# Expert matrices kept interleaved in SBUF, and read by the products with a step of eight values

## The chip, the core and the metric

One core of a Trainium2 chip runs the whole program. The metric is device time in microseconds (us) of one execution, given as the median of several runs. Five engines work beside each other and are tied by semaphores alone: TensorE (PE, with its weight loads listed as PEld), VectorE (DVE), ScalarE (ACT), GpSimd (POOL) and SyncE (SP), which here issues most of the DMAs.

## What is computed

An attention block and a feed-forward block with eight experts, each followed by a layer norm. Only the second half of the program is touched by the change:

```python
x = layernorm(x + attention(x))                  # x: 8 x 512 tokens of 512 values
logits = clip(xt @ gate_w.T)                     # 8 experts
top_w, top_idx = top_k(logits, 2)
rw = softmax(top_w)
deltas = softmax(expert_atom_weights) @ atoms    # 8 x 4096
weighted = deltas * sigmoid(importance)
vals = einsum('tk,tks->ts', rw, weighted[top_idx])
contrib = segment_sum((xt[:, cols] * vals).T, rows)   # rows, cols: from mask_idx
x = layernorm(x + xt @ W.T + contrib.T)
```

The kernel writes the sparse part of each expert into a dense 512 x 512 matrix, together with `W` and the identity, so that a token's result is the sum of two products, one with each chosen expert's matrix, weighted by `rw`.

## The kernel before

The stages run one after the other: `expert_entries` (the sparse entries), `attention` (most of the time; it also routes the tokens of all batches but the last), `experts` and `combine`. The eight experts' matrices lie in DRAM as `expert_weights`, with the expert as the innermost index: for each row and column the values of the eight experts lie side by side.

`experts` has two halves. In the first, the preparation, SyncE loads the matrices into SBUF in eight parts of 128 partitions x 2048 values (256 columns times 8 experts), into a ring of three slots called `stage`. Products are made in float32r, and each factor is split in a high part (the value rounded to float32r) and a low part (the rest), so that three products of parts stand for one. For each part and each expert ScalarE casts 256 values, read from `stage` with a step of eight, into `d_hi` (line 1558), where the experts lie apart; then VectorE (line 1621, function `lows`) or GpSimd (line 1433) subtracts `d_hi` from the same values in `stage` and writes `d_lo`. `DVE_E` (line 1396) shares this: VectorE has four of eight experts in parts 0 to 3 and all of them in parts 4 to 7. A slot of the ring is loaded again when both have finished with it (lines 1412 and 1413).

Between these, VectorE finishes the last 512 tokens: their layer norm, their logits (by TensorE from `x1T`, which ScalarE copies behind part 0), their two best experts, and their places in the table `expert_slots`, which GpSimd scatters in eight small DMAs behind part 3. In the program of VectorE the order is `lows(0)`, logits, `lows(1)`, choice of experts, `lows(2)`, places, `lows(3)`, `lows(4)`, counts of tiles, `lows(5)`, the tiles' experts, `lows(6)`, tile numbers, `lows(7)`, token numbers (line 1707). SyncE loads the table (`slots`, line 1420) when the scatter has landed; the token numbers need it.

The second half is a loop over 72 tiles of 128 tokens of one expert, in turns of four. GpSimd fetches the 128 rows of a tile with an indirect DMA (line 1458) and, for an earlier tile, sends the result's rows with another (line 1464). TensorE turns the fetched rows (four transposes, line 1523); ScalarE and VectorE split them into `xT_hi` and `xT_lo`; TensorE then makes twelve products of 128 x 128 by 128 x 512 (lines 1534 to 1536), whose moving operand is the tile's expert in `d_hi` or `d_lo`, picked by a register; ScalarE scales the result. TensorE turns the next tile's rows ahead of the products of this one. TensorE and GpSimd both enter the loop only when all of `d_lo` is there.

Of the kernel before, what the change touches and what calls it, by code (L numbers as in the profile page):

```python
# [27 lines left out]
P = 128  # L28
# [1310 lines left out]
def experts(nc, sem, s_passed, psum, ident, upper, ones, R, rows, gate_w, d_dram, y_dram):  # L1339

    LAST = NT - TT
    with ExitStack() as ctx:
        def sb(name, shape, dt=F32):
            return ctx.enter_context(nc.sbuf_tensor(name, shape, dt))

        d_hi, d_lo = sb("d_hi", [P, C, NE, DM], F32R), sb("d_lo", [P, C, NE, DM], F32R)

        STAGES = 3
        stage = sb("stage", [P, STAGES, DM * NE // 2])
# [43 lines left out]
        block = ctx.enter_context(nc.Block())  # L1393
        PARTS = 2 * C

        DVE_E = [NE // 2] * (PARTS // 2) + [NE] * (PARTS - PARTS // 2)

        def part(q, e):

            return stage[:, q % STAGES].rearrange("p (r e) -> p e r", e=NE)[:, e]  # L1400

        def place(w, q, e):
            return w[:, q // 2, e, (q % 2) * (DM // 2):(q % 2 + 1) * (DM // 2)]

        @block.sync
        def _(sp):
            sp.dma_start(gate_rows[:], gate_w).then_inc(s_gate_in, 16)
            weights = d_dram[0:DM * DM, :].rearrange("(c p h r) e -> c h p (r e)", c=C, p=P, h=2)
            for q in range(PARTS):
                if q >= STAGES:  # L1410

                    sp.wait_ge(s_d_lo, sum(DVE_E[:q - STAGES + 1]))
                    sp.wait_ge(s_d_lo_pool, NE * (q - STAGES + 1) - sum(DVE_E[:q - STAGES + 1]))
                sp.dma_start(stage[:, q % STAGES], weights[q // 2, q % 2]).then_inc(s_d_in[q % STAGES], 16)
                if q == 3:
                    sp.wait_ge(s_x1, TT)
                    sp.dma_start(R.x1_dram[LAST * P:, :].rearrange("(t p) d -> p t d", p=P), rows[:]).then_inc(s_x1_out, 16)

            sp.wait_ge(R.s_placed, 32 * (NT + 1))
            sp.dma_start(slots[:].rearrange("p n a -> p (n a)"), R.table.rearrange("(p n) a -> p (n a)", p=P)).then_inc(s_ids_in, 16)  # L1420
            for k in range(GROUP):

                sp.wait_ge(s_y_out[k], 16 * TURNS)

        @block.gpsimd
        def _(pool):
# [1 line left out]
            pool.wait_ge(s_var, 1)  # L1428
            pool.tensor_tensor(rstd[:], var_eps[:], R.minus_half[:], ALU.pow).then_inc(s_rstd, 1)
            for q in range(PARTS):  # L1430
                for e in range(DVE_E[q], NE):
                    pool.wait_ge(s_d_hi, q * NE + e + 1)
                    pool.tensor_tensor(place(d_lo, q, e), part(q, e), place(d_hi, q, e).bitcast(F32),
                                       ALU.subtract).then_inc(s_d_lo_pool, 1)
                if q == PARTS // 2 - 1:

                    pool.wait_ge(s_place, 1)
                    for t in range(TT):
                        for k in range(2):
                            pool.indirect_dma_start(  # L1440
                                out=R.table, out_offset=bass.IndirectOffsetOnAxis(ap=place_tile[:, t, k:k + 1], axis=0),
                                in_=last_slot[:, t, k], in_offset=None).then_inc(R.s_placed, 16)

            pool.wait_ge(s_ids, 1)
            pool.wait_ge(s_x1_out, 16)
            pool.wait_ge(s_d_lo, sum(DVE_E))
            pool.wait_ge(s_tiles, 1)

            def fetch(j, k, buf, sent):
# [36 lines left out]
        def _(pe):  # L1486
# [27 lines left out]
            pe.matmul(psum[:, 1, 0:NE], ones[:], before[:, TT], start=True, stop=True).then_inc(s_counts, 1)  # L1514

            pe.wait_ge(s_tiles, 1)
            pe.wait_ge(s_d_lo, sum(DVE_E))
            pe.wait_ge(s_d_lo_pool, NE * PARTS - sum(DVE_E))

            def turn(j, k, loaded):  # L1520
                pe.wait_ge(s_tok_in[k], loaded)
# [4 lines left out]
            def multiply(j, k):  # L1526
                e = pe.value_load(tile_expert_i[0:1, bass.ds(j, 1)], min_val=0, max_val=NE - 1)
                pe.wait_ge(s_lo, j + 1)

                dst = psum[:, 4 + k, :]  # L1530
                for c in range(C):
                    hi = d_hi[:, c, bass.ds(e, 1), :].rearrange("p a n -> p (a n)")
                    lo = d_lo[:, c, bass.ds(e, 1), :].rearrange("p a n -> p (a n)")
                    pe.matmul(dst, xT_hi[:, k % 2, c], hi, start=c == 0, stop=False)
                    pe.matmul(dst, xT_hi[:, k % 2, c], lo, start=False, stop=False)
                    last = pe.matmul(dst, xT_lo[:, k % 2, c], hi, start=False, stop=c == C - 1)
                last.then_inc(s_y, 1)
# [16 lines left out]
        def _(act):  # L1554
            for q in range(PARTS):
                act.wait_ge(s_d_in[q % STAGES], 16 * (q // STAGES + 1))
                for e in range(NE):
                    act.copy(place(d_hi, q, e), part(q, e)).then_inc(s_d_hi, 1)
                if q == 0:
                    for c in range(C):  # L1560
                        act.wait_ge(s_x1T_pe, c + 1)
                        act.copy(x1T[:, c], psum[:, 4 + c, :]).then_inc(s_x1T, 1)
                if q == 2:
                    act.wait_ge(s_gap, 1)
                    act.activation(gap[:, 1], gap[:, 0], ACT.Exp).then_inc(s_gap_exp, 1)
# [25 lines left out]
        def _(dve):  # L1591
# [24 lines left out]

            def lows(q):

                for e in range(DVE_E[q]):
                    dve.wait_ge(s_d_hi, q * NE + e + 1)  # L1620
                    dve.tensor_tensor(place(d_lo, q, e), part(q, e), place(d_hi, q, e).bitcast(F32),
                                      ALU.subtract).then_inc(s_d_lo, 1)

            lows(0)
# [242 lines left out]
```

## Time and profile before

| | us |
|---|---|
| median of three runs | 2079.24 (2078.22 to 2080.32) |
| the profiled execution, its own time | 2079.65 |
| its span in the trace | 2078.1 |
| TensorE busy | 1845.8 (89%) |
| VectorE busy | 1188.1 (57%) |
| ScalarE busy | 816.1 (39%) |
| GpSimd busy | 793.4 (38%) |

The span is what the trace covers, from the first to the last recorded work; the execution's own time is a little longer. Busy times are sums over the whole span, in which the attention takes the greater part; for a change in one stage the stretch of that stage has to be read by itself. The experts' preparation runs from about 1688 to 1755 us, the loop over the tiles from there to 2002, and the combining stage to the end. In the rows, a start is given in us from the span's start; products show some 0.39 us each although they start more closely, since they overlap, so their pace is the distance of starts.

### The profile page before, as it was taken

Reading aid. Unit: us, or ns where it says so; the run is one execution under the profiler, and the core shown is the slowest. Engines: PE = TensorE matmul, PEld = TensorE weight load, DVE = VectorE, ACT = ScalarE, POOL = GpSimd, SP = SyncE. Lnnn points to the kernel's source line nnn. Section 1 sums busy time; section 2 is a strip of 40 time slices with the busy share of each in tenths; the row PEclk is TensorE's granted clock in tenths of the full one; section 3 lists DMA queues with packets and bytes.
Section 4 is the critical chain, followed back from the end, with each engine's and each line's share of the span. In section 5 each row is a group of like instructions: output and inputs, shape, how many; then the busy total and the mean of one; then the engine's idle time right before and its main releaser. Section 6 shows DMA issues by size and latency. Waiting matters only on the chain. (4 is left out here: it accounts for less than half of the span.)

```text
span 2078.1 us, 35224 instructions
## 1 busy us (share of the span) xinstructions
PE 1845.8 (89%) x9447; PEld 1549.2 (75%) x9448; DVE 1188.1 (57%) x3710; ACT 816.1 (39%) x2038; POOL 793.4 (38%) x1242
## 2 busy tenths in 40 slices
PE   6899999999999999999999999999999842999950
PEld 6788788878887888788878887888788732877740
DVE  4445446665666566656656665676567756222237
ACT  1244434434443343444434443444344443333324
POOL 5366423223232333233323332333233333666643
PEclk6899999999999999999999999999999975999975
DMA  9453353323333433243324333333324133444458
GB/s 316 158 167 117 112 190 106 116 98 132 116 106 101 142 101 106 96 142 106 111 94 139 111 104 119 121 107 138 124 74 141 52 122 104 149 156 148 146 210 364
DMA packets 113037, 278.74 MB, mean 134 GB/s; under 512 B 17808, under 2 KB 28064, under 8 KB 103016
## 3 DMA queue, kind: packets, MB, share of 16 engines
q1 hardware_dynamic: 92128, 229.03, 31.7%
q0 software_dynamic: 20816, 48.73, 7.4%
q8 instruction: 26, 0.43, 0.1%
q14 instruction: 67, 0.55, 0.1%
HBM read 207.00 MB, written 70.72 MB: 134 GB/s over the span
## 5 line engine op out<-in xcount | busy, mean ns | idle before, releaser
L847 POOL TENSOR_SCALAR probs<-probs,row_inv 128x128 f32<-128x128 f32 (+3 forms) x512 | 275.7, 584 | 471.3 <-DVE row_inv L1220 466.8
L1127 ACT ACTIVATE probs<-probs,neg_max 128x512 f32<-128x512 f32 (+3 forms) x512 | 283.2, 556 | 410.2 <-DVE neg_max L1212 397.4
L924 PE MATMUL psum<-xT_hi,w_hi 128*128 128x512 f32 x640 | 257.4, 402 | 23.4 <-DVE qT_lo L1233 10.6
L926 PE MATMUL psum<-xT_hi,w_lo 128*128 128x512 f32 x640 | 251.5, 393 | 0.0
L925 PE MATMUL psum<-xT_lo,w_hi 128*128 128x512 f32 x640 | 250.9, 392 | 0.0
L1212 DVE CUSTOM_DVE_ANT_0 probs<-psum,causal 128x512 f32<-128x512 f32 (+3 forms) x512 | 222.8, 487 | 46.5 <-PE psum L926 20.3
L1223 DVE TENSOR_TENSOR pT_lo<-psum,pT_hi 128x512 fp32r<-128x512 f32 (+1 forms) x384 | 206.5, 594 | 9.6 <-ACT pT_hi L1137 9.6
L924 PE MATMUL psum<-wo_hi,oT_hi 128*128 128x512 f32 x512 | 202.7, 396 | 1.4 <-DVE oT_lo L1223 1.4
L926 PE MATMUL psum<-wo_hi,oT_lo 128*128 128x512 f32 x512 | 200.3, 391 | 0.0
L925 PE MATMUL psum<-wo_lo,oT_hi 128*128 128x512 f32 x512 | 199.6, 390 | 0.0
L1137 ACT CAST pT_hi<-psum 128x512 fp32r<-128x512 f32 (+1 forms) x384 | 172.9, 529 | 61.5 <-PE psum L951 61.5
L1233 DVE SCALAR_TENSOR_TENSOR qT_lo<-psum,qT_hi 128x512 fp32r<-128x512 f32 x128 | 88.5, 691 | 169.1 <-ACT qT_hi L1141 169.1
L924 PE MATMUL psum<-kT_hi,qT_hi 128*128 128x512 f32 (+3 forms) x512 | 170.1, 332 | 2.9 <-issue 1.5
L924 PE MATMUL psum<-pT_hi,v_hi 128*128 128x512 f32 (+1 forms) x384 | 142.5, 371 | 26.2 <-DVE xT_lo L352 24.5
L925 PE MATMUL psum<-kT_lo,qT_hi 128*128 128x512 f32 (+3 forms) x512 | 164.9, 322 | 0.0
L924 PEld LDWEIGHTS psum<-xT_hi,w_hi 128*128 128x128 f32 x640 | 120.6, 188 | 59.2 <-DVE qT_lo L1233 13.4
L926 PE MATMUL psum<-kT_hi,qT_lo 128*128 128x512 f32 (+3 forms) x512 | 164.5, 321 | 0.0
L951 PE MATMUL psum<-ident,probs 128*128 128x128 f32 x1280 | 160.7, 273 | 2.6 <-DVE pT_lo L1223 2.6
L951 PEld LDWEIGHTS psum<-ident,probs 128*128 128x128 f32 x1280 | 147.4, 141 | 19.9 <-issue 3.2
L1141 ACT ACTIVATE qT_hi<-psum 128x512 fp32r<-128x512 f32 x128 | 76.2, 596 | 207.8 <-PE psum L926 205.6
L267 DVE CUSTOM_DVE_ANT_0 route_product<-route_rows,route_gate 128x512 f32<-128x512 f32 x224 | 151.2, 684 | 0.0
L1223 DVE TENSOR_TENSOR oT_lo<-psum,oT_hi 128x512 fp32r<-128x512 f32 x128 | 88.4, 691 | 102.0 <-ACT oT_hi L1150 102.0
(248 smaller groups left out, 3813.0 us busy)
## 6 DMA issues: line engine op xcount, KB each, us to landing
w_hi<-split_qk_weights SPq DMA_DIRECT2D x140, 256.0 KB, 2.7
w_lo<-split_qk_weights SPq DMA_DIRECT2D x140, 256.0 KB, 2.9
wo_hi<-split_out_weights SPq DMA_DIRECT2D x28, 1024.0 KB, 5.0
wo_lo<-split_out_weights SPq DMA_DIRECT2D x28, 1024.0 KB, 7.1
c_y<-chosen_rows SPq DMA_DIRECT2D x32, 512.0 KB, 9.1
x_in<-in_L_attn_x_dram SPq DMA_DIRECT2D x8, 1024.0 KB, 6.5
expert_weights<-fill_sb SPq DMA_DIRECT2D x4, 2048.0 KB, 9.2
stage<-expert_weights SPq DMA_DIRECT2D x8, 1024.0 KB, 7.0
```

The lines of the kernel that those rows point to most:

```text
L267: dve.tensor_tensor_reduce(R.product[:, e % 2], R.rows[:], R.gate[:, e], 1.0, 0.0, ALU.mult, ALU.add, R.logits[:, e:e + 1]).then_inc(R.s_c ...
L847: last = pool.tensor_scalar(p, p, row_inv[:, buf, i:i + 1], 1.0, ALU.mult, ALU.mult)
L924: pe.matmul(dst, hi_s, hi_m, start=start, stop=False)
L925: pe.matmul(dst, hi_s, lo_m, start=False, stop=False)
L926: return pe.matmul(dst, lo_s, hi_m, start=False, stop=stop)
L951: last = pe.transpose(psum[:, BANKS_PT[unit], at:at + P], probs[:, buf, src:src + P], ident[:])
L1127: last = act.activation(probs[:, buf, a:a + w], probs[:, buf, a:a + w], ACT.Exp, bias=neg_max[:, buf, i:i + 1], scale=-1.0, accum_out=row_ ...
L1137: act.copy(pT_hi[:, buf, a:z], psum[:, BANKS_PT[u], 0:z - a]).then_inc(s_pt_hi, 1)
L1141: act.mul(qT_hi[:, buf], psum[:, BANK_A, :], SCALE).then_inc(s_q_hi, 1)
L1212: last = dve.tensor_tensor_reduce(probs[:, buf, a:a + w], psum[:, BANK_S + bank, col:col + w], causal[:, T - w:T], -1.0, -MASKED, ALU.add, ...
L1223: dve.tensor_tensor(lo, src, hi.bitcast(F32), ALU.subtract).then_inc(done, 1)
L1233: dve.scalar_tensor_tensor(out=qT_lo[:, buf], in0=psum[:, BANK_A, :], scalar=SCALE, in1=qT_hi[:, buf].bitcast(F32), op0=ALU.mult, op1=ALU. ...
```

## The change

`d_hi` and `d_lo` are laid out like the matrices in DRAM, with the expert innermost. The split then works on whole parts: one cast of 2048 adjacent values on ScalarE, and one subtraction of 2048 adjacent values, on VectorE for parts 0, 2, 4, 5, 6 and 7 and on GpSimd for parts 1 and 3. The waits count parts instead of experts. The products take their 512 moving values from `d_hi` and `d_lo` with a step of eight, beginning at the expert's number. Nothing else is different.

```diff
--- before.py
+++ after.py
@@ -1343,7 +1343,7 @@
         def sb(name, shape, dt=F32):
             return ctx.enter_context(nc.sbuf_tensor(name, shape, dt))
 
-        d_hi, d_lo = sb("d_hi", [P, C, NE, DM], F32R), sb("d_lo", [P, C, NE, DM], F32R)
+        d_hi, d_lo = sb("d_hi", [P, C, DM, NE], F32R), sb("d_lo", [P, C, DM, NE], F32R)
 
         STAGES = 3
         stage = sb("stage", [P, STAGES, DM * NE // 2])
@@ -1393,14 +1393,14 @@
         block = ctx.enter_context(nc.Block())
         PARTS = 2 * C
 
-        DVE_E = [NE // 2] * (PARTS // 2) + [NE] * (PARTS - PARTS // 2)
-
-        def part(q, e):
-
-            return stage[:, q % STAGES].rearrange("p (r e) -> p e r", e=NE)[:, e]
-
-        def place(w, q, e):
-            return w[:, q // 2, e, (q % 2) * (DM // 2):(q % 2 + 1) * (DM // 2)]
+        DVE_PARTS = [q for q in range(PARTS) if q not in (1, 3)]
+
+        def part(q):
+
+            return stage[:, q % STAGES]
+
+        def place(w, q):
+            return w[:, q // 2, (q % 2) * (DM // 2):(q % 2 + 1) * (DM // 2)].rearrange("p r e -> p (r e)")
 
         @block.sync
         def _(sp):
@@ -1409,8 +1409,10 @@
             for q in range(PARTS):
                 if q >= STAGES:
 
-                    sp.wait_ge(s_d_lo, sum(DVE_E[:q - STAGES + 1]))
-                    sp.wait_ge(s_d_lo_pool, NE * (q - STAGES + 1) - sum(DVE_E[:q - STAGES + 1]))
+                    if q - STAGES in DVE_PARTS:
+                        sp.wait_ge(s_d_lo, DVE_PARTS.index(q - STAGES) + 1)
+                    else:
+                        sp.wait_ge(s_d_lo_pool, (1, 3).index(q - STAGES) + 1)
                 sp.dma_start(stage[:, q % STAGES], weights[q // 2, q % 2]).then_inc(s_d_in[q % STAGES], 16)
                 if q == 3:
                     sp.wait_ge(s_x1, TT)
@@ -1428,9 +1430,9 @@
             pool.wait_ge(s_var, 1)
             pool.tensor_tensor(rstd[:], var_eps[:], R.minus_half[:], ALU.pow).then_inc(s_rstd, 1)
             for q in range(PARTS):
-                for e in range(DVE_E[q], NE):
-                    pool.wait_ge(s_d_hi, q * NE + e + 1)
-                    pool.tensor_tensor(place(d_lo, q, e), part(q, e), place(d_hi, q, e).bitcast(F32),
+                if q not in DVE_PARTS:
+                    pool.wait_ge(s_d_hi, q + 1)
+                    pool.tensor_tensor(place(d_lo, q), part(q), place(d_hi, q).bitcast(F32),
                                        ALU.subtract).then_inc(s_d_lo_pool, 1)
                 if q == PARTS // 2 - 1:
 
@@ -1443,7 +1445,7 @@
 
             pool.wait_ge(s_ids, 1)
             pool.wait_ge(s_x1_out, 16)
-            pool.wait_ge(s_d_lo, sum(DVE_E))
+            pool.wait_ge(s_d_lo, len(DVE_PARTS))
             pool.wait_ge(s_tiles, 1)
 
             def fetch(j, k, buf, sent):
@@ -1514,8 +1516,8 @@
             pe.matmul(psum[:, 1, 0:NE], ones[:], before[:, TT], start=True, stop=True).then_inc(s_counts, 1)
 
             pe.wait_ge(s_tiles, 1)
-            pe.wait_ge(s_d_lo, sum(DVE_E))
-            pe.wait_ge(s_d_lo_pool, NE * PARTS - sum(DVE_E))
+            pe.wait_ge(s_d_lo, len(DVE_PARTS))
+            pe.wait_ge(s_d_lo_pool, PARTS - len(DVE_PARTS))
 
             def turn(j, k, loaded):
                 pe.wait_ge(s_tok_in[k], loaded)
@@ -1529,8 +1531,8 @@
 
                 dst = psum[:, 4 + k, :]
                 for c in range(C):
-                    hi = d_hi[:, c, bass.ds(e, 1), :].rearrange("p a n -> p (a n)")
-                    lo = d_lo[:, c, bass.ds(e, 1), :].rearrange("p a n -> p (a n)")
+                    hi = d_hi[:, c, :, bass.ds(e, 1)].rearrange("p n a -> p (n a)")
+                    lo = d_lo[:, c, :, bass.ds(e, 1)].rearrange("p n a -> p (n a)")
                     pe.matmul(dst, xT_hi[:, k % 2, c], hi, start=c == 0, stop=False)
                     pe.matmul(dst, xT_hi[:, k % 2, c], lo, start=False, stop=False)
                     last = pe.matmul(dst, xT_lo[:, k % 2, c], hi, start=False, stop=c == C - 1)
@@ -1554,8 +1556,7 @@
         def _(act):
             for q in range(PARTS):
                 act.wait_ge(s_d_in[q % STAGES], 16 * (q // STAGES + 1))
-                for e in range(NE):
-                    act.copy(place(d_hi, q, e), part(q, e)).then_inc(s_d_hi, 1)
+                act.copy(place(d_hi, q), part(q)).then_inc(s_d_hi, 1)
                 if q == 0:
                     for c in range(C):
                         act.wait_ge(s_x1T_pe, c + 1)
@@ -1616,9 +1617,9 @@
 
             def lows(q):
 
-                for e in range(DVE_E[q]):
-                    dve.wait_ge(s_d_hi, q * NE + e + 1)
-                    dve.tensor_tensor(place(d_lo, q, e), part(q, e), place(d_hi, q, e).bitcast(F32),
+                if q in DVE_PARTS:
+                    dve.wait_ge(s_d_hi, q + 1)
+                    dve.tensor_tensor(place(d_lo, q), part(q), place(d_hi, q).bitcast(F32),
                                       ALU.subtract).then_inc(s_d_lo, 1)
 
             lows(0)
```

## Rows read from the trace of the kernel before

**Rows 1.** Stretches: length, busy PE, PEld, DVE, ACT, POOL, granted clock, DMA share, GB/s.

```profile
15.70:20.00 4.30, 3.69 (x32) 3.60 (x32) 1.78 (x5) 0.39 (x1) 4.30 (x2) 0.50 0.97 394
...
26.50:41.00 14.50, 14.03 (x65) 13.94 (x64) 1.68 (x3) 2.49 (x2) 8.27 (x7) 0.50 0.94 391
...
1690.00:1755.00 65.00, 10.45 (x40) 6.58 (x40) 48.56 (x143) 38.61 (x70) 29.53 (x36) 0.55 0.46 155
1755.90:1758.60 2.70, 2.69 (x6) 2.15 (x7) 0.75 (x2) 0.57 (x1) 1.86 (x5) 0.50 0.40 124
...
1762.00:2002.30 240.30, 231.60 (x1123) 184.83 (x1121) 52.30 (x139) 82.78 (x139) 155.77 (x269) 1.00 0.45 149
```

**Rows 2.** Timeline of TensorE in the loop: start, length, line, operands.

```profile
1757.35 0.63 PE L1534 MATMUL psum<-d_hi,tokT_hi 128*128 x1
...
1757.78 0.63 PE L1535 MATMUL psum<-d_lo,tokT_hi 128*128 x1
...
1795.32 0.60 PE L1523 MATMUL psum<-ident,stage 128*128 128x128 f32 x4
...
1799.20 0.39 PE L1535 MATMUL psum<-d_lo,tokT_hi 128*128 x1
1799.43 0.39 PE L1536 MATMUL psum<-d_hi,tokT_lo 128*128 x1
...
1801.72 0.60 PE L1523 MATMUL psum<-ident,stage 128*128 128x128 f32 x4
```

**Rows 3.** GpSimd's fetches, line 1458, from 1740 to 2003 us.

```profile
L1458 POOL DMA_INDIRECT stage<-x,ids_now x72: 975/986/1027, 1749.1 to 1991.7; - x72
```

**Rows 4.** Instructions by line, 1690 to 2005 us: count | busy us, mean ns | idle before.

```profile
L1534 PE MATMUL psum<-d_hi,tokT_hi 128*128 x288 | 120.0, 417 | 4.2 <-issue 4.2
...
L1464 POOL DMA_INDIRECT chosen_rows<-stage,dest_now x72 | 71.0, 987 | 28.8 <-issue 21.6 <-ACT stage L1582 7.2
...
L1558 ACT CAST d_hi<-stage 128x256 fp32r<-128x256 f32 x64 | 36.2, 653 | 28.6 <-DMA stage<-expert_weights 28.5
...
L1621 DVE TENSOR_TENSOR d_lo<-stage,d_hi 128x256 fp32r<-128x256 f32 x48 | 25.7, 604 | 0.3 <-ACT d_hi L1558 0.3
L1433 POOL TENSOR_TENSOR d_lo<-stage,d_hi 128x256 fp32r<-128x256 f32 x16 | 15.1, 984 | 7.6 <-ACT d_hi L1558 7.6
```

**Rows 5.** Waits from 1756 to 2003 us: total, times, longest.

```profile
PEld psum L1523 <- DMA stage<-x,ids_now: 10.4, 14, 1.6
```

**Rows 6.** Instructions by line, whole span: the same work on adjacent values.

```profile
L607 DVE TENSOR_TENSOR wv_lo<-wo_raw,wv_hi 128x2048 fp32r<-128x2048 f32 x1 | 2.3, 2293 | 0.1
...
L536 ACT CAST wv_hi<-wo_raw 128x2048 fp32r<-128x2048 f32 x1 | 1.9, 1899 | 1.9 <-DMA wo_raw<-in_L_attn_wv_dram 1.9
...
L830 POOL TENSOR_TENSOR v_lo<-v_raw,v_hi 128x512 fp32r<-128x512 f32 x32 | 41.5, 1296 | 6.0 <-POOL v_hi L825 6.0
```

**Rows 7.** Timeline of the preparation: ScalarE, VectorE and SyncE.

```profile
1697.68 2.02 ACT L1562 COPY x1T<-psum 128x512 f32<-128x512 f32 x4
...
1715.51 2.22 DVE L1621 TENSOR_TENSOR d_lo<-stage,d_hi 128x256 fp32r<-128x256 f32 x4 [0.25 <-ACT d_hi L1558]
...
1720.16 6.33 DVE L1621 TENSOR_TENSOR d_lo<-stage,d_hi 128x256 fp32r<-128x256 f32 x12
...
1728.81 4.26 DVE L1621 TENSOR_TENSOR d_lo<-stage,d_hi 128x256 fp32r<-128x256 f32 x8
...
1732.94 0.32 SPq L1420 DMA_DIRECT2D slots<-expert_slots  x1
...
1746.50 0.29 DVE L1707 TENSOR_SCALAR token_ids<-slots 128x256 int32<-128x256 int32 x1
```

**Rows 8.** DMA issues of the page: KB each, median us to landing.

```profile
stage<-expert_weights SPq DMA_DIRECT2D x8, 1024.0 KB, 7.0
```

**Rows 9.** Timeline of weight loads: importance rows (step 32 values) and gate rows (adjacent).

```profile
15.72 3.60 PEld L490 LDWEIGHTS psum<-ident,imp_sb 8*128 8x128 f32 x32 [2.81 <-DMA imp_sb<-in_L_ffn_importance_dram]
...
1689.43 0.50 PEld L1490 LDWEIGHTS psum<-ident,gate_rows 8*128 8x128 f32 x4 [9.10 <-DMA gate_rows<-in_L_ffn_gate_w_dram]
```

## The prediction

> **What bounds the kernel now.** The edit touches one stage, the experts, so I read the stretches first [rows 1]. From 1690 to 1755 us TensorE is busy 10.45 of 65 us while VectorE is busy 48.56: this is the preparation, in which the experts' matrices are split into a high and a low part. From 1762 to 2002.3 us TensorE is busy 231.6 of 240.3 us at the full clock: this is the loop over 72 token tiles. Everything before and after keeps its code.
>
> In the loop, look at two paces. TensorE's own is in its timeline [rows 2]: from one tile's transposes at 1795.32 to those two tiles later at 1801.72, 3.20 us per tile, with twelve products in it, one started every 0.23 us in mid-tile. Four transposes and the change between the two kinds are the other 0.44. GpSimd's pace is in its row of fetches [rows 3]: 72 of them from 1749.1 to 1991.7, (1991.7 - 1749.1) / 71 = 3.42 us per tile, made of a fetch of 0.99, a send of 0.99 [rows 3, 4] and the time to issue them. So GpSimd is the slower of the two by 0.22 us per tile, although TensorE shows 96% busy; TensorE waits for the fetched rows only in little pieces, 14 waits of 10.4 us in all on its weight queue [rows 5]. The loop from the first product at 1755.9 to the last at 2002.3 takes 246.4 us = 72 x 3.42. A product may thus grow by 0.22 / 12 = 18 ns before anything is seen.
>
> **Part 1, the preparation.** It removes 64 casts on ScalarE (36.2 us busy, 0.565 each), 48 subtractions on VectorE (25.7, 0.535 each) and 16 on GpSimd (15.1, 0.94 each), all of 256 values read with a step of eight [rows 4]. It adds 8, 6 and 2 of 2048 adjacent values. Rows of that kind stand elsewhere in this trace: a cast of 128x2048 on ScalarE takes 1.90 us, a subtraction of 128x2048 on VectorE 2.29, one of 128x512 on GpSimd 1.30, so 5.2 for four times that [rows 6]. New busy times: ScalarE 15.2, VectorE 13.8, GpSimd 10.4.
>
> On the path is VectorE: its work runs almost without a gap to the token numbers at 1746.50 [rows 7], which release GpSimd's first fetch. Behind the last layer norm, 44 of its 48 subtractions lie in that chain: 44 x 0.535 = 23.5 us become five pieces (parts 2, 4, 5, 6, 7), 11.5 us: 12 off. The turned tokens x1T are copied by ScalarE behind its first eight casts, at 1697.68 [rows 7]; those took 8 x 0.565 = 4.5 and become one of 1.9, so the routing of the last tokens starts 2.6 earlier. Against that: with three stage slots, part 5 is loaded only when part 2 is subtracted. Part 2 begins at 1715.5 [rows 7]; it comes 2.6 + 2.1 (part 1's four subtractions, now GpSimd's) earlier, at 1710.8, and ends at 1713.1. A load takes 7.0 [rows 8], the cast 1.9, so part 5 is there at 1722.0. VectorE comes to it at 1728.8 - 2.6 - 2.1 - 4.0 (twelve subtractions of parts 3 and 4, 6.3, become one of 2.3) = 1720.1 [rows 7] and waits 1.9. Sum: -12 - 2.6 + 1.9 = -13 us.
>
> Bounds. The slots' load starts at 1732.94 [rows 7], behind the scatter of the last tokens; it moves up by about 5, not 13, to 1728. With under half the 7.0 us that a load of four times its size takes to land, the token numbers can't come before about 1731: at most -15. The small end: GpSimd's pieces of parts 1 and 3 are 5.2 us long each; the loads of parts 4 and 6 wait for them, and if VectorE's chain met three quarters of both, 8 us would be lost: -5. A loss is excluded, since each of the three engines has less to do. No wait is new: VectorE and GpSimd waited per expert for the cast and now wait per part, with the routing steps queued behind, as before.
>
> **Part 2, the products.** Their count (three lines of 288 [rows 4]), their stationary operands, their sizes and the register that picks the expert stay. What changes is that the 512 moving values lie eight values apart. No row before has a product that reads so; the price has to be bounded.
>
> From below: TensorE does read strided operands once, as weights. The 32 loads of the importance rows (line 490, a step of 32 values) take 3.60 us, 0.112 each; the four loads of adjacent gate rows of the same 8x128 take 0.50, 0.125 each [rows 9]. No price is seen there. But this was at a granted clock of 0.50 [rows 1], with 128 values in 0.112 us, 0.88 ns per value. A product at the full clock takes a value every 0.23 / 512 = 0.45 ns. So the row shows that 0.88 ns per strided value can be had, and is silent on twice that rate. Low end: no price. A gain is excluded, since the product itself has no less to do.
>
> From above: ScalarE and VectorE read the very same pattern in the casts and subtractions [rows 4], 0.565 / 256 = 2.2 ns and 2.1 ns per value; for adjacent values they take 1.90 / 2048 = 0.93 and 1.12 [rows 6]. That is 2.4 and 1.9 times as long, with a fixed part in the short ones: both engines look like going at half rate. At VectorE's 2.1 ns a product would take 1.07 us; that is the far end, which the weight loads at 0.88 ns speak against.
>
> I take half rate for TensorE too, that is the pitch it has at the lower clock, 0.43 us (from 1757.35 to 1757.78) [rows 2]: 0.84 ns per value, next to the 0.88 that the weight loads show as possible. Price 0.20 us per product.
>
> The Trainium skill (Advanced Engine Details and Errata, SBUF Cachelines) says that SBUF is read in 16-byte lines, that two hits on a line are needed to absorb the access latency, and that a new line for each access is penalised, without a size. The rows of ScalarE and VectorE agree with it, 2.4 and 1.9 times; the weight loads at half clock show no such penalty. By the page a product pays something, by the weight loads alone nothing, and the time would be that of the first rival.
>
> At a price of 0.20 a tile takes 3.20 + 12 x 0.20 = 5.60 us on TensorE, GpSimd's 3.42 is hidden, and the loop is 72 x 5.60 = 403 us instead of 246.4: +157. (864 x 0.20 = 173 would count the 16 us in which TensorE now waits for GpSimd's pace.) Some six products at the start already run at the lower clock [rows 1], an uncertainty of 2 us. GpSimd, ScalarE and VectorE get more slack in the loop; the send of the last tile and the combining stage behind it stay as long.
>
> **Sum.** +157 - 13 = +144 on the profiled execution's own 2079.65 us (span 2078.1): 2223.7. The median of the three runs is 0.4 lower, so 2223. With the pitch between 0.42 and 0.44 (9 us either way) and the preparation between -15 and -5 this case reaches from 2205 to 2243.
>
> **Rivals.**
> Free steps: TensorE takes a strided value at every cycle of the full clock too. Then GpSimd's 3.42 still sets the loop, 246 us, and only the preparation counts: 2079.2 - 13 = 2066. For it: the weight loads without a price. Against it: the two other engines, and that the weight loads ran at half clock.
> By the Trainium skill (TensorE: Matmul & The Clock Gate, Step-by-step: what each phase is for) one column enters the array per cycle and throughput is purely the number of columns; taken as it stands it makes this rival the result.
>
> A partial price, between 18 ns and 0.20. The change turns from gain to loss where the loop gives back the 13 us: 13 / 864 = 15 ns above the hidden 18, at a pitch of about 0.26. At 1.5 times (0.345) the loop is 72 x (3.20 + 12 x 0.115) = 330, so +83 - 13: 2149. Nothing in the rows gives such a ratio but GpSimd, which reads 3.7 ns against 2.5.
>
> The clock falls as well: in the loop of slower products TensorE is granted the lower of its two levels, 1.2 instead of 2.4 GHz. A busy engine is no proof against it: from 26.5 to 41 us, with weight loads and short products, it is busy for 14.03 of 14.5 us and granted 0.50; in the loop as it is it is granted 1.00 [rows 1]. If a value then still costs two cycles, a product takes 0.86 and the rest of a tile 0.88: 72 x (12 x 0.86 + 0.88) = 806, +560 - 13: 2626. If the price is a time and not a number of cycles, only the transposes grow, +32: 2255.
>
> The preparation doesn't shorten because the parts wait for their loads: 2236, inside the first case's range.
>
> **How the numbers follow.** Half rate 0.64, free 0.18, fallen clock (2255 to 2626) 0.10, a partial price 0.08. A measurement of this kernel can tell about 0.2%, 4 us, from no change. Faster: the free case, 0.18. Within: a partial price near 0.26 pitch, 0.02. Slower: the rest, 0.80. The first case and the partial one hold 0.72; to leave out no more than 0.2 the range has to reach down to the free case, with its preparation at -15: 2060. The top is the first case's end with a little for the transposes, 2250. The first case alone: 2205 to 2243.
>
> **What would show it.** In the loop: starts of products 0.43 apart and transposes 5.6 apart at a granted clock of 1.00; no more wait of TensorE for fetched rows, and GpSimd waiting for ScalarE's results. Ahead of it: eight casts of 1.9 us, six subtractions of 2.3, token numbers near 1734. A pitch still at 0.23 makes the forecast wrong as a whole (2066); 0.43 with a loop start that hasn't moved makes only part 1 wrong; a clock of 0.50 in the loop is the third rival.

## The result and the profile after

The changed kernel takes 2227.53 us (median of 4 runs, 2226.57 to 2229.76) where the kernel before takes 2078.73 (4 runs): a ratio of 1.0716, 95% interval 1.0698 to 1.0735, or +149 us. The forecast was 2223. The profiled execution's own time is 2227.55, its span 2225.9.

Stretches of the kernel after, with the columns of [rows 1]:

```profile
1690.00:1742.00 52.00, 9.08 (x34) 5.59 (x34) 35.41 (x94) 17.38 (x13) 26.86 (x16) 0.57 0.50 179
...
1746.00:2148.00 402.00, 401.92 (x1143) 206.14 (x1143) 53.87 (x143) 82.64 (x142) 158.74 (x276) 0.99 0.28 91
```

The second line is the loop: TensorE is busy 401.92 of 402 us at a granted clock of 0.99, where 8.7 us of 240.3 were free before [rows 1]. VectorE, ScalarE and GpSimd do what they did, in 1.6 times as long (403.4 us for 246.4, see below). Ahead of it the preparation is shorter, and VectorE's 48.56 us of 65 [rows 1] are 35.41 of 52.

TensorE's timeline of the kernel after, in the loop, as [rows 2], and then at the loop's beginning, with the stretch that holds it:

```profile
1802.85 0.62 PE L1525 MATMUL psum<-ident,stage 128*128 128x128 f32 x4
...
1803.70 0.62 PE L1537 MATMUL psum<-d_lo,tokT_hi 128*128 x1
1804.13 0.62 PE L1538 MATMUL psum<-d_hi,tokT_lo 128*128 x1
...
1808.46 0.62 PE L1525 MATMUL psum<-ident,stage 128*128 128x128 f32 x4
```

```profile
1747.60 0.62 PE L1537 MATMUL psum<-d_lo,tokT_hi 128*128 x1
1748.03 0.61 PE L1538 MATMUL psum<-d_hi,tokT_lo 128*128 x1
```

```profile
1747.00:1750.50 3.50, 3.50 (x8) 2.66 (x9) 0.75 (x2) 0.54 (x1) 2.18 (x6) 0.50 0.39 116
```

Products start 0.43 us apart (1803.70, 1804.13) instead of 0.23, and a tile takes 1808.46 - 1802.85 = 5.61 us. The second fence adds something: here the clock is still at 0.50 (stretch 1747 to 1750.5), and the distance is 0.43 as well, which is also what adjacent values take at this clock [rows 2]. The step of eight costs nothing at the lower level, and at the higher one it takes back just what the clock gives.

Instructions by line of the kernel after, 1680 to 2160 us, columns as in [rows 4]:

```profile
L1536 PE MATMUL psum<-d_hi,tokT_hi 128*128 x288 | 182.1, 632 | 0.1
...
L1466 POOL DMA_INDIRECT chosen_rows<-stage,dest_now x72 | 70.7, 982 | 184.7 <-ACT stage L1583 177.8 <-issue 6.9
...
L1442 POOL DMA_INDIRECT expert_slots<-last_slot,last_place_tile x8 | 15.2, 1896 | 8.2 <-DVE last_place_tile L1673 6.1 <-issue 2.1
L1559 ACT CAST d_hi<-stage 128x2048 fp32r<-128x2048 f32 x8 | 15.1, 1897 | 36.2 <-DMA stage<-expert_weights 36.2
L1622 DVE TENSOR_TENSOR d_lo<-stage,d_hi 128x2048 fp32r<-128x2048 f32 x6 | 13.7, 2288 | 1.2 <-ACT d_hi L1559 1.1
L1435 POOL TENSOR_TENSOR d_lo<-stage,d_hi 128x2048 fp32r<-128x2048 f32 x2 | 9.0, 4502 | 10.3 <-ACT d_hi L1559 10.3
L1646 DVE COPY chosen_before<-route_counts 128x8 f32<-128x8 f32 x1 | 4.4, 4406 | 0.0
```

GpSimd, which set the loop's pace [rows 3], now sits idle 177.8 us ahead of its sends until ScalarE has results. The casts and subtractions take what [rows 6] promised: 15.1 for 36.2 us, 13.7 for 25.7, 9.0 for 15.1 [rows 4]. But the last line stands out: a copy of eight values that takes 4.4 us.

The books, from first product to end. Loop: 1747.00 to 2150.44 (the last product starts at 2149.82 and lasts 0.62), 403.4 us for 246.4: +157.0. First product: 1747.00 for 1755.91 [rows 1], -8.9, of which 0.8 came with the stage (its first load is issued at 1686.89 instead of 1687.68); so the preparation gave 8.1, not 13. Behind the loop 75.5 us for 75.8. Sum 157.0 - 8.9 - 0.3 = 147.8, the difference of the two spans.

The missing 5 us are seen in the timeline of the preparation of the kernel after (in brackets, what ended the wait before):

```profile
1700.45 0.68 DVE L1627 COPY logitsT<-psum 8x512 f32<-8x512 f32 x1 [3.74 <-PE psum L1504]
...
1706.00 4.50 POOL L1435 TENSOR_TENSOR d_lo<-stage,d_hi 128x2048 fp32r<-128x2048 f32 x1 [2.13 <-ACT d_hi L1559]
1706.12 4.41 DVE L1646 COPY chosen_before<-route_counts 128x8 f32<-128x8 f32 x1
...
1727.20 2.29 DVE L1622 TENSOR_TENSOR d_lo<-stage,d_hi 128x2048 fp32r<-128x2048 f32 x1
1727.25 3.08 POOL L1442 DMA_INDIRECT expert_slots<-last_slot,last_place_tile  x1 [0.30 <-issue]
1730.63 0.96 POOL L1442 DMA_INDIRECT expert_slots<-last_slot,last_place_tile  x1 [0.31 <-issue]
1730.78 2.28 DVE L1622 TENSOR_TENSOR d_lo<-stage,d_hi 128x2048 fp32r<-128x2048 f32 x1
...
1735.07 0.32 SPq L1422 DMA_DIRECT2D slots<-expert_slots  x1
1737.66 0.29 DVE L1708 TENSOR_SCALAR token_ids<-slots 128x256 int32<-128x256 int32 x1 [4.60 <-DMA slots<-expert_slots]
```

Read it in pairs. The copy of eight values starts 0.12 us behind GpSimd's subtraction and ends at 1710.53, when that ends (1710.50). A scatter issue that starts behind the beginning of one of VectorE's subtractions ends 0.8 us after it (1730.33 and 1729.49); of the eight, five are held like that. One that starts 0.15 us ahead of such a subtraction (1730.63 and 1730.78) takes 0.96 in all. Eight issues take 15.2 us for 9.1 before, the slots' load starts at 1735.07 and not at 1728 as forecast, and VectorE waits 4.60 us for it. VectorE's own last subtraction ends at 1733.06.

The copy's hold is not part of the loss, since the kernel before has the like of it in smaller pieces. From `last_gap` to `last_share_sum`, small steps of VectorE that run beside GpSimd's subtractions, it takes 9.7 us (1705.36 to 1715.09), and the changed kernel 9.2 (1702.26 to 1711.43). New is the scatter's hold: from its first start to its last end it takes 17.3 us, for 11.2 before.

### The profile page after: what moved, and what is told of

It is laid out like the page before. It is cut to its first block and busy times, and to the rows that moved or that the text cites. A ratio compares the mean times of both kernels' runs of the same rounds, so it can differ in the third digit from the quotient of the medians.

```text
span 2225.9 us, 35107 instructions
## 1 busy us (share of the span) xinstructions
PE 2010.3 (90%) x9447; PEld 1565.0 (70%) x9448; DVE 1175.7 (53%) x3668; ACT 792.4 (36%) x1982; POOL 791.5 (36%) x1228
## 5 line engine op out<-in xcount | busy, mean ns | idle before, releaser
L1713 DVE COPY share_now<-slots 128x1 f32 x72 | 11.1, 154 | 349.7 <-ACT tokT_hi L1571 296.9
L1536 PE MATMUL psum<-d_hi,tokT_hi 128*128 x288 | 182.1, 632 | 0.1
L1538 PE MATMUL psum<-d_hi,tokT_lo 128*128 x288 | 178.7, 620 | 0.0
L1537 PE MATMUL psum<-d_lo,tokT_hi 128*128 x288 | 178.6, 620 | 0.0
L1583 ACT ACTIVATE stage<-psum,share_now 128x512 f32<-128x512 f32 x72 | 49.5, 687 | 320.9 <-PE psum L1538 320.9
```

## The experiments

The first four ask where the loss is and what exactly costs it; then weights, pieces, writes.

### Reading adjacent values from the new layout

```diff
-                    hi = d_hi[:, c, :, bass.ds(e, 1)].rearrange("p n a -> p (n a)")
+                    hi = d_hi[:, c].rearrange("p r e -> p (r e)").rearrange("p (a n) -> p a n", n=DM)[:, bass.ds(e, 1)].rearrange("p a n -> p (a n)")
```

(`lo` likewise.) 

> The changed kernel, but the products read 512 adjacent values (which mixes experts and columns, so the result is not the reference's). Theory, the step of eight costs all of the loss: products start 0.23 us apart again, the loop is paced by GpSimd at 3.42 us per tile, 246 us, and what is left is the preparation alone: 2078.7 - 9 = about 2070. Rival, the interleaved layout or the shorter preparation harms the loop in another way (transfers or subtractions that collide): more than 2079.

2068.08 us against 2079.71 (ratio 0.9944, 0.9928 to 0.9961). Line 1536 is back at 417 ns for 632, products start 0.23 us apart, and the loop takes 246.5 us. So the whole loss is the step's, and the preparation by itself is a gain: -11.6 us by the medians (interval -15.0 to -8.1). The trace gives -8.2 for the preparation, with a first product at 1746.38 and a stage that begins 1.3 us earlier; these 1.3 are not the preparation's.

### The step alone, in the kernel before

```diff
-                    hi = d_hi[:, c, bass.ds(e, 1), :].rearrange("p a n -> p (a n)")
+                    hi = d_hi[:, c].rearrange("p e n -> p (e n)").rearrange("p (n a) -> p n a", a=NE)[:, :, bass.ds(e, 1)].rearrange("p n a -> p (n a)")
```

(`lo` likewise.) 

> The kernel before, its split and layout untouched, but the products read with a step of eight across the experts (so the values multiplied are the wrong ones). Theory, the price is the step's alone: 0.43 us per product, 5.61 per tile, loop 404 instead of 246, so 2078.7 + 157 = 2236, some 8 above the changed kernel. Rival, the price comes with the way the values were written or with the shorter preparation: pitch below 0.40 and a time under 2200.

2237.09 us, ratio 1.0758 (1.074 to 1.0776), +157.4. TensorE's timeline in the loop:

```profile
1803.24 0.62 PE L1523 MATMUL psum<-ident,stage 128*128 128x128 f32 x4
...
1804.09 0.62 PE L1535 MATMUL psum<-d_lo,tokT_hi 128*128 x1
1804.52 0.62 PE L1536 MATMUL psum<-d_hi,tokT_lo 128*128 x1
...
1808.85 0.40 PE L1523 MATMUL psum<-ident,stage 128*128 128x128 f32 x2
```

The same 0.43 and 5.61. Who wrote the matrices, and in what pieces, doesn't matter. The two runs are two halves of the change: +157.4 and -11.6 make +145.8; the whole measured +148.8, and 3 us are within the intervals.

### Which steps pay

In the changed kernel, chunk c of each tile (three products each) reads with a step of c + 1 values.

```diff
+                    def stepped(w):
+                        rows8 = w[:].rearrange("p c r e -> p (c r e)").rearrange("p (a m) -> p a m", a=NE)
+                        return rows8[:, bass.ds(e, 1), 0:DM * (c + 1):c + 1].rearrange("p a n -> p (a n)")
+                    hi, lo = stepped(d_hi), stepped(d_lo)
```

> The changed kernel with the products of the four chunks of a tile read at steps of 1, 2, 3 and 4 values (not the reference's values): the pitch of each step can be read in one loop. Theory A, half rate for every step above one: 0.23, 0.43, 0.43, 0.43, a tile of 5.0 us. Theory B, a price for each new line of 16 bytes when only one value of it is used (the Trainium skill, Advanced Engine Details and Errata, SBUF Cachelines: two hits on a line absorb it): 0.23 at a step of 2, 0.43 at a step of 4, between them at 3 (a tile of about 4.0 to 4.2 us). Theory C, the price grows with the distance: 2, 3 and 4 in even stages.

2198.72 us (one run). TensorE's timeline over one tile; after the transposes (at 1802.02) come three products of step 1, 2, 3 and 4 in turn, at a granted clock of 1.00:

```profile
1802.71 0.39 PE L1539 MATMUL psum<-d_lo,tokT_hi 128*128 x1
1802.94 0.39 PE L1540 MATMUL psum<-d_hi,tokT_lo 128*128 x1
...
1803.61 0.63 PE L1539 MATMUL psum<-d_lo,tokT_hi 128*128 x1
1804.06 0.63 PE L1540 MATMUL psum<-d_hi,tokT_lo 128*128 x1
...
1805.85 0.65 PE L1538 MATMUL psum<-d_hi,tokT_hi 128*128 x1
1806.31 0.65 PE L1539 MATMUL psum<-d_lo,tokT_hi 128*128 x1
```

Step 1: 0.23. Step 2: 0.45 (1803.61 to 1804.06), and step 3 the same. Step 4: 0.46. The price doesn't grow with the step; a step of 2 pays it in full. The Trainium skill (Advanced Engine Details and Errata, SBUF Cachelines) asks for two hits on a 16-byte line; a step of 2 makes two, and pays nevertheless. The page's rule is too mild for these products.

### Groups of adjacent values

The next kernel reads pairs (values 0 and 1 of every eight), pairs across a 16-byte border (3 and 4), single values with a step of 16, and fours (0 to 3 of every eight), in chunks 0 to 3.

```diff
+                        if c == 2:
+                            return flat[:, 0:DM * 16:16]
+                        first, count = ((0, 2), (3, 2), None, (0, 4))[c]
+                        groups = flat.rearrange("p (a g t) -> p a g t", a=NE, t=8)[:, bass.ds(e, 1), 0:DM // count, first:first + count]
```

> The changed kernel with the four chunks' products reading, in this order: pairs of adjacent values eight apart, starting at 0; the same pairs starting at 3, so that a pair lies across a border of 16 bytes; single values with a step of 16; groups of four adjacent values eight apart (not the reference's values). Theory A, each jump costs once: pairs 0.33, pairs at 3 0.33, step 16 0.43, fours 0.28. Theory B, price only for a line of 16 bytes of which one value is used: pairs 0.23, pairs across the border 0.43, step 16 0.43, fours 0.23. Theory C, the price grows with the distance: step 16 above 0.5.

2198.55 us (one run). In the timeline, fours of one tile and then pairs of the next:

```profile
1803.66 0.39 PE L1543 MATMUL psum<-d_lo,tokT_hi 128*128 x1
1803.89 0.40 PE L1544 MATMUL psum<-d_hi,tokT_lo 128*128 x1
...
1804.98 0.66 PE L1543 MATMUL psum<-d_lo,tokT_hi 128*128 x1
1805.44 0.66 PE L1544 MATMUL psum<-d_hi,tokT_lo 128*128 x1
```

Pairs 0.46 apart, pairs across the border 0.46, step 16 0.43, fours 0.23 (the first of them 0.27). So fours are free and pairs are not, whether a border lies in them or not. That left a question: must the four lie within one 16-byte group?

### Where a four may lie

Chunk 0 reads fours that straddle a border (2 to 5 of every eight), chunk 1 eights (0 to 7 of every sixteen), chunk 2 fours (0 to 3 of every 32), chunk 3 adjacent values from the second on.

```diff
+                        if c == 3:
+                            return flat.rearrange("p (a m) -> p a m", a=NE)[:, bass.ds(e, 1), 1:DM + 1].rearrange("p a n -> p (a n)")
+                        every, first, count = ((8, 2, 4), (16, 0, 8), (32, 0, 4))[c]
```

> The changed kernel with the four chunks' products reading: fours of adjacent values eight apart, beginning at value 2 of eight; eights of adjacent values sixteen apart; fours 32 apart; and 512 adjacent values beginning one value later (not the reference's values). Theory A, what counts is that four adjacent values follow each other: all four chunks at 0.23. Theory B, the four must lie in one line of 16 bytes: fours at 2 at 0.45, the shifted adjacent values at 0.23 to 0.3, the others 0.23. Theory C, jumps are the price and longer runs pay fewer: fours 0.25 to 0.3, eights less.

2105.97 us (one run). TensorE's timeline over one tile, chunks 0 to 3 in turn:

```profile
1804.00 0.65 PE L1545 MATMUL psum<-d_lo,tokT_hi 128*128 x1
1804.45 0.65 PE L1546 MATMUL psum<-d_hi,tokT_lo 128*128 x1
...
1805.17 0.39 PE L1545 MATMUL psum<-d_lo,tokT_hi 128*128 x1
1805.40 0.40 PE L1546 MATMUL psum<-d_hi,tokT_lo 128*128 x1
1805.64 0.42 PE L1544 MATMUL psum<-d_hi,tokT_hi 128*128 128x512 f32 x1
1805.89 0.42 PE L1545 MATMUL psum<-d_lo,tokT_hi 128*128 128x512 f32 x1
...
1806.64 0.40 PE L1545 MATMUL psum<-d_lo,tokT_hi 128*128 x1
1806.88 0.40 PE L1546 MATMUL psum<-d_hi,tokT_lo 128*128 x1
```

Straddling fours 0.45, eights 0.23, aligned fours far apart 0.25, shifted adjacent values 0.24. So it is the aligned group of four fp32 values that TensorE reads at full speed. Taken over these runs: 512 values in 128 or 129 such groups take 0.23 to 0.25 us; from 256 groups (pairs, straddling fours, step 2) 0.45 to 0.46; from 384 (step 3) 0.45; from 512 (steps 4, 8 and 16, pairs across the border) 0.43 to 0.46. It isn't a price per group, since 512 cost no more than 256.

### Weights with a step

In the kernel before, the turned tokens are read as weights with a step of four values; the products' moving operands stay adjacent.

```diff
+                    x_hi = xT_hi[:, k % 2].rearrange("p c n -> p (c n)")[:, c:C * P:C]
+                    x_lo = xT_lo[:, k % 2].rearrange("p c n -> p (c n)")[:, c:C * P:C]
```

> The kernel before with the products' weights (the turned tokens) read at a step of four values instead of adjacent (the tokens of a tile are mixed, so not the reference's values); the moving values stay adjacent. It asks whether a strided weight load costs something at the full clock, where the row of the importance loads was silent. Theory, weight loads have no price: 0.19 us each, products 0.23 apart, 2079. Rival, they go at half rate like the moving values: loads longer by 0.05 to 0.11 us; products stay 0.23 apart as long as a load hides under a product, otherwise 0.3.

2080.7 us (one run) against 2079.14. One line of the weight queue, this kernel's and then, in the second fence, the one of the kernel before:

```profile
L1537 PEld LDWEIGHTS psum<-d_lo,tokT_hi 128*128 128x128 f32 x288 | 91.1, 316 | 0.2
```

```profile
L1535 PEld LDWEIGHTS psum<-d_lo,tokT_hi 128*128 128x128 f32 x288 | 54.8, 190 | 9.4
```

A load with a step shows 316 ns for 190 at the full clock. (The three lines add up to 270 us in a loop of 248, so these records overlap; 316 ns is a length, not a pace.) It lies beside the running product but for the first of a tile, which comes 0.13 us later; a tile grows from 3.20 to 3.37 and stays under GpSimd's 3.42 [rows 3], so the total shows next to nothing. At a granted clock of 0.50, at the loop's beginning, the same loads show 0.33 us with the step (at 1756.14) as without it (the kernel before, at 1756.93). So the loads of [rows 9], from which the lower bound of the prediction came, stood at a clock at which no price can be seen.

### VectorE's subtractions in pieces

The changed kernel, with each of VectorE's subtractions cut into eight of 256 adjacent values.

```diff
+                    for h in range(8):
+                        piece = slice(h * N, (h + 1) * N)
+                        last = dve.tensor_tensor(place(d_lo, q)[:, piece], part(q)[:, piece],
+                                                 place(d_hi, q)[:, piece].bitcast(F32), ALU.subtract)
```

> The changed kernel with each of VectorE's subtractions of 2048 adjacent values cut into eight of 256. Theory, VectorE's long two-input instructions hold up GpSimd's issue of the eight scatters (17.3 us instead of 11.2), which makes the slots' load late: the scatters come back to 11 to 12 us, the token numbers at about 1734.5 instead of 1737.7, 2224.5 in all, although VectorE has some 1.5 us more to do. Rival, the scatter's issue is slow for another reason: scatters still 15 us or more, token numbers no earlier than 1737, 2228 to 2230.

2226.32 us, ratio 1.0711 (1.0693 to 1.0729). Instructions by line and the timeline:

```profile
L1442 POOL DMA_INDIRECT expert_slots<-last_slot,last_place_tile x8 | 8.3, 1042 | 9.1 <-DVE last_place_tile L1677 6.9 <-issue 2.1
```

```profile
1728.62 0.32 SPq L1422 DMA_DIRECT2D slots<-expert_slots  x1
1734.95 0.28 DVE L1712 TENSOR_SCALAR token_ids<-slots 128x256 int32<-128x256 int32 x1
```

The scatter takes 8.3 us for 15.2 and the slots' load starts 6.5 us earlier (0.4 of them come with the stage), near the 1728 of the forecast: long subtractions on VectorE did hold up the scatter. But the token numbers come only 2.7 earlier, since VectorE itself is now last (no wait is shown at its line): its pieces take 16.6 us in all for 13.7. By the medians the gain is 1 us, within the two intervals.

### Both engines' subtractions in pieces

As above, and GpSimd's two subtractions in eight pieces each as well. 

> The changed kernel with VectorE's and GpSimd's subtractions all cut into pieces of 256 adjacent values. Theory, what was missing of the preparation's 13 us is the mutual holding up: one VectorE copy of 8 values took 4.41 us beside GpSimd's subtraction; cut up, it takes under 1 us and the token numbers come at 1731 to 1733 instead of 1737.7 (1734.95 with VectorE's pieces alone), 2222 to 2224 in all. Rival, GpSimd's pieces meet more of VectorE's small steps and nothing is won over VectorE's pieces alone: 1735 and later, 2226.

2225.28 us, ratio 1.0698 (1.0681 to 1.0715). The copy of eight values takes 0.62 us for 4.41:

```profile
L1654 DVE COPY chosen_before<-route_counts 128x8 f32<-128x8 f32 x1 | 0.6, 625 | 0.0
```

So it was GpSimd's long subtraction that held it. Its neighbours take over a part of the hold: from `last_gap` to `last_share_sum` VectorE needs 7.7 us, for 8.1 with its own pieces alone and 9.2 in the changed kernel. The token numbers come at 1733.65, 47.7 us behind the stage's first load, where the kernel with VectorE alone in pieces has 48.5, the changed kernel 50.8 and the kernel before 58.8. Both holds are thus real, and removing them is worth 3 us in the trace, 2.3 of it by VectorE's pieces; the times of the last two kernels don't tell them apart.

### Strided writes in place of strided reads

Could the layout of before be kept, so that products read adjacent values, and the preparation still work on whole parts? ScalarE makes the high part twice, once in the order of the weights (for the subtractions, in a new buffer of two slots) and once placed; casts and subtractions read adjacent values and write with a step of 512.

```diff
-                for e in range(NE):
-                    act.copy(place(d_hi, q, e), part(q, e)).then_inc(s_d_hi, 1)
+                act.copy(high_of(q), part(q)).then_inc(s_d_hi, 1)
...
+                act.copy(place(d_hi, q), part(q)).then_inc(s_x1T, 1)
```

> A third layout of the work: the experts lie apart as in the kernel before, so products read adjacent values; the parts are 2048 wide as in the changed kernel, with VectorE and GpSimd reading adjacent values (a second, interleaved copy of the high part is kept for them) and writing with a step of 512. It asks what a strided write costs. Theory A, a strided write has no price: subtractions 2.3 us, ScalarE's placing casts 1.9, token numbers near 1738, about 2069. Theory B, writes go at half rate like reads: subtractions 4.3, placing casts 3.6 and more, and then no gain over the kernel before: 2077 to 2085.

2076.67 us (10 runs) against 2079.14, ratio 0.9989 (0.998 to 0.9999). Instructions by line:

```profile
L1580 ACT CAST d_hi<-stage 128x2048 fp32r<-128x2048 f32 x8 | 29.6, 3698 | 0.0
L1636 DVE TENSOR_TENSOR d_lo<-stage,high_part 128x2048 fp32r<-128x2048 f32 x6 | 22.3, 3715 | 0.8 <-ACT high_part L1572 0.7
L1447 POOL DMA_INDIRECT expert_slots<-last_slot,last_place_tile x8 | 16.9, 2112 | 4.9 <-DVE last_place_tile L1687 2.7 <-issue 2.1
...
L1440 POOL TENSOR_TENSOR d_lo<-stage,high_part 128x2048 fp32r<-128x2048 f32 x2 | 9.1, 4552 | 18.5 <-ACT high_part L1572 18.5
L1668 DVE TENSOR_SCALAR last_share_sum<-last_gap 128x4 f32<-128x4 f32 x1 | 4.5, 4510 | 0.0
```

Writes with a step pay too: a cast 3.70 us for 1.90, a subtraction on VectorE 3.72 for 2.29; GpSimd's takes 4.55 for 4.50, no more. With the two engines holding each other as well (16.9 us of scatter, 4.5 for four values), the token numbers come at 1745.20 for 1746.50 [rows 7], and little is left.

### The same in pieces

VectorE's subtractions in four, GpSimd's in eight pieces. 

> The third layout (adjacent reads, strided writes) with VectorE's subtractions cut in four and GpSimd's two in eight. Theory, VectorE and GpSimd hold each other up for whole instructions of two SBUF inputs: without the pieces two VectorE steps of 0.2 us stood at 4.51 and 4.04 us behind GpSimd's subtractions, and the scatter took 16.9 us busy; cut up, the two steps come back under 1 us, the scatter to 9 to 12 us, the token numbers from 1745.2 to about 1738, 2069 to 2071 in all. Rival, the pieces only add fixed parts and the chain waits for ScalarE's casts all the same: 2076 to 2079.

2075.51 us (11 runs) against 2080.29, ratio 0.9976 (0.9967 to 0.9985): the fastest version of the whole work here, 5 us ahead of the kernel before; less than expected, and a little faster than the rival's 2076. The scatter is down to 10.1 us, but the long holds became many short ones (eight small steps of VectorE, one line, 692 ns each, for 226 in the changed kernel), and VectorE's chain, with 22.3 us of subtractions for 25.7 before [rows 4], is still what ends last: the token numbers wait for nothing at 1743.78, in a stage that began 1.5 us later than before.

## Why the prediction was right, and where a term was off

**What bounds the kernel.** Right. GpSimd's 3.42 us hid a part of the price exactly as worked out: 157 us and not 173. With a tile at 5.60, GpSimd is the one that waits.

**Part 2, the price of a product.** Right in size, 0.20 us, and the loop to 0.2 us (403 forecast, 403.4 measured; +157 and +157.0). The choice of half rate rested on ScalarE and VectorE and was an analogy; the runs with the step alone and the step removed make it a measurement. The bound from below was blind, as the prediction suspected: its row stood at the lower clock, where neither a weight load (0.33 us with and without a step of four) nor a product (0.43 with and without a step of eight) pays for a step. The reason was less sure than the number. The Trainium skill's 16-byte lines gave the direction, and their length is that of the group that decides here, but two hits on one are not enough: it has to be read whole.

**The rivals.** Free steps fell with the run of the step alone. The Trainium skill (TensorE: Matmul & The Clock Gate, Step-by-step: what each phase is for) counts one column per cycle; here 512 columns take 0.23 us in whole groups and 0.43 to 0.46 otherwise, at the same clock. A partial price fell with the steps of 2 to 4: no layout that was tried lies between 0.25 and 0.43 in mid-chunk. The clock didn't fall (0.99), and the first products show what the 2626 of that rival would have got wrong: at the lower level a product with a step of eight takes no longer than an adjacent one, so that the price is a time per value, about 0.84 ns, not two cycles of whatever clock is granted.

**Part 1, the preparation.** The term that was mis-sized: -13 forecast, -8.1 in the trace (-8.1 to -15.0 by the times of the kernel that reads adjacent values; -9.6 by the medians of the changed kernel and the one with the step alone). The cost of each cast and subtraction was right, and GpSimd's 4.50 was even below the 5.2 estimated. The step that failed is "it moves up by about 5, not 13, to 1728", said of the slots' load: each edit was costed by its own length, and VectorE's long subtractions were not free for GpSimd's scatter. Against the stage's first load, it starts 2.9 us later than before instead of 5 earlier. With VectorE's subtractions cut in pieces it starts at 1728.62, with GpSimd's as well at 1727.30.

Taken by its steps, the -13 was right in its largest and lucky in two others. VectorE's chain from the copy of the logits (1702.04 before, the line below; 1700.45 after) to the end of its last subtraction shrank from 44.5 to 32.6 us, -11.9 for the -12. The routing starts only 0.8 us earlier against the stage's start, not 2.6: the casts ahead of ScalarE's copies of x1T did get shorter, but TensorE, busy 3.6 us with transposes and 3.6 with the logits' products, had waited only 0.8 us for these copies. And VectorE hardly waits for part 5, 0.1 us at most and not 1.9. These two errors cancel, and what is left are the 4.6 us of waiting for the slots' load: -11.9 - 0.8 + 4.6 = -8.1.

```profile
1702.04 0.68 DVE L1626 COPY logitsT<-psum 8x512 f32<-8x512 f32 x1 [5.75 <-PE psum L1502]
```

With both engines' subtractions in pieces the token numbers come 11.1 us earlier than before, against the stage's first load. That the remaining 2 us to the forecast are the pieces' own overhead (17.2 us for 13.7 on VectorE) is argued from their busy time, not tried.

**Sum.** +157.0, -8.9 and -0.3 against +157 and -13: the profiled execution's own time was put at 2223.7 and is 2227.55, and the 3.9 us between them are this one term, 4.9 off, less the 0.8 by which the stage began earlier and the 0.3 behind the loop. The prediction's lower end of its first case, 2205, doesn't come out of its terms (2223 less 9, 2 and 2 is 2210); nothing hung on it.

## What to carry to other kernels

Before a layout is turned so that its writer is quick, count who reads it and how often: here whole-part splits saved 8 to 12 us, and 864 products with a step cost 157. For TensorE's fp32r moving operand keep at least four adjacent values on a 16-byte boundary; a layout with experts side by side in groups of four values per expert would be read at 0.25 us per product (the fours of every 32 above); a kernel written for it was not tried. And when short instructions are merged into long ones on VectorE or GpSimd, look at what the other of the two has to start meanwhile: a row's price is its own length plus the hold.

## What the runs showed of the hardware

- At the full clock a product of 512 moving fp32r values takes 0.23 to 0.25 us when they come in whole aligned groups of four or as one adjacent run, also one that begins a value later, and 0.43 to 0.46 in any other layout tried (steps 2, 3, 4, 8, 16, pairs, straddling fours). At a granted clock of 0.50 it takes 0.43 with adjacent values and with a step of eight. Why steps of 8 and 16 are a little cheaper (0.43) than steps of 2 to 4 and pairs (0.45 to 0.46) stays open.
- Weight loads with a step of four: 0.31 us for 0.19 at the full clock, 0.33 for 0.33 at a granted clock of 0.50.
- Writes with a step of 512 values cost ScalarE 1.95 times, VectorE 1.62 times, GpSimd nothing (4.55 for 4.50 us).
- Small VectorE instructions that read SBUF (copies, casts, steps with one or two inputs) and start beside a two-input subtraction of GpSimd can end only with it: 4.41 us for a copy of eight values, 0.62 beside pieces. Not all do: beside the first subtraction (1699.36 to 1703.87) a step that reads PSUM and four MAX8 take 0.19 us and, together, 0.37 (0.17 and 0.37 in the kernel before). GpSimd's scatter issues that start beside a two-input subtraction of VectorE in the changed kernel end 0.8 to 0.9 us after it. The Trainium skill (SBUF — State Buffer, Who interferes with whom) lists copies and such subtractions among what can contend with GpSimd, and infers that the subtractions leave descriptor generation alone. Here issues beside them take up to 3.1 us instead of 0.96; since an issue also reads its places from SBUF, whether that read or the descriptors had to wait stays open.
